# Attention's side work placed by half slots, with PSUM readers between the exponentials, and the second phase's square root moved up

## The reference, cut to what matters

```python
# block 1: attention, 16 heads of 8
zn = (z - mu) / sqrt(var + EPS) * ln_scale + ln_bias
q, k, v = split(zn @ w_qkv)
att = softmax(q @ k.T / sqrt(8))            # 512 x 512 for each head
return z + (att @ v) @ w_proj + b_proj
# block 2: quantised feed-forward
x_q = (x / s_in).astype(float8_e4m3fn)
return (x_q @ k_q * s_in * s_k).astype(bf16) + bias
# block 3: gated recurrence (convolution, gates, scan), then a gated MLP
beta = sqrt(1.0 - alpha ** 2 + 1e-06)
xs = beta * sigmoid(inp) * xc
h = associative_scan(alpha, xs)
return x + gelu(mgate) * mx @ W_shrink.T
# block 4: routing of tokens to 8 experts
```

## Time and profile before

| what | before |
|---|---|
| median of 3 runs | 1431.36 us (1431.35 to 1436.4) |
| the profiled execution | 1437.65 us |
| its span, first to last instruction | 1435.9 us |
| mean granted PE clock | 0.943 of full speed |
| PE busy | 1220.5 us (85%) |
| DVE busy | 1160.6 us (81%) |
| ACT busy | 968.2 us (67%) |
| POOL busy | 824.6 us (57%) |

### The profile page before, as it was taken

How to read it: one execution, slowest core, us unless ns; L and a number is a source line. 1 busy time by engine, 2 the same in 40 slices (tenths; PEclk the granted TensorE clock), 3 DMA queues, 4 the chain that set the end, 5 groups by cost and what they waited for, 6 DMA issues and landing times.

```text
span 1435.9 us, 26041 instructions
## 1 busy us (share of the span) xinstructions
PE 1220.5 (85%) x8624; PEld 492.4 (34%) x8624; DVE 1160.6 (81%) x2518; ACT 968.2 (67%) x1653; POOL 824.6 (57%) x1068
## 2 busy tenths in 40 slices
PE   1499899899899999999999999856999899899853
PEld 0123233233233233233233223323545545545533
DVE  2668889889889889889989988433789889889874
ACT  1177777777777777877877878555767667666630
POOL 5303554654654654655555444634677877877763
PEclk7589999999999999999999989888999999999975
DMA  1121101101101101101100100000000000000000
GB/s 56 50 83 42 35 31 42 36 31 41 37 31 42 37 31 40 38 30 41 39 30 32 34 14 3 1 0 1 1 8 16 8 8 16 8 8 16 8 8 22
DMA packets 52517, 37.87 MB, mean 26 GB/s; under 512 B 8864, under 2 KB 51744, under 8 KB 52384
## 3 DMA queue, kind: packets, MB, share of 16 engines
q1 hardware_dynamic: 52384, 36.22, 7.9%
HBM read 6.31 MB, written 4.19 MB: 7 GB/s over the span
## 4 chain that ended last, share of the span: by engine, by line
PE 33%; DVE 23%; POOL 20%; issue 13%; SPq 5%; ACT 5%; POOLq 0%; DMA 0%; ACTq 0%; DVEq 0%
DVE neg_max L473 11%; PE bank L201 10%; PE bank L182 9%; SPq L621 4%; PE bank_pair L169 4%; ACT probs L348 3%; PE bank L210 3%; POOL probs L1154 2%; PE bank L272 2%; POOL x_all L1148 2%; POOL zn L1146 1%; POOL rs_t L1088 1%; POOL probs L1119 1%; POOL rs_x L1088 1%; POOL rs_h L1116 1%
## 5 line engine op out<-in xcount | busy, mean ns | idle before, releaser
L473 DVE TENSOR_REDUCE neg_max<-bank_pair 128x2 f32<-128x1024 f32 x512 | 615.5, 1215 | 120.7 <-PE bank_pair L169 115.9
L348 ACT ACTIVATE probs<-bank 128x512 f32<-128x512 f32 x1024 | 558.5, 596 | 113.2 <-PE bank L182 108.6
L182 PE MATMUL bank<-q_stack,k_stack 50*128 50x512 bf16 x1024 | 362.3, 390 | 36.4 <-ACT probs L348 19.3
L201 PE MATMUL bank<-probs,v_pad 128*32 128x256 f32 x4096 | 331.4, 396 | 2.7 <-ACT outT L306 2.3
L169 PE MATMUL bank_pair<-k_stack,q_stack 48*128 48x512 bf16 x1024 | 293.8, 397 | 31.0 <-DMA k_stack<-k_parts 15.7
L182 PEld LDWEIGHTS bank<-q_stack,k_stack 50*128 50x128 bf16 x1024 | 83.6, 93 | 301.2 <-ACT probs L348 228.6
L201 PEld LDWEIGHTS bank<-probs,v_pad 128*32 128x32 f32 x4096 | 81.1, 108 | 175.6 <-issue 156.0
L724 PE MATMUL bank_pair<-probs,w_gates 128*128 128x512 f32 x256 | 122.7, 624 | 16.7 <-DVE probs L1046 8.9
L522 POOL TENSOR_TENSOR f_b<-f_bf,ffn_bias 128x512 bf16<-128x512 bf16 x16 | 18.9, 1182 | 157.3 <-ACT f_bf L353 157.3
L169 PEld LDWEIGHTS bank_pair<-k_stack,q_stack 48*128 48x128 bf16 x1024 | 54.0, 94 | 60.5 <-DVE neg_max L473 41.2
L1154 POOL TENSOR_TENSOR probs<-probs 128x1024 f32<-128x1024 f32 x16 | 37.7, 2354 | 62.9 <-DVE probs L1068 62.9
(11 more groups left out here) (232 smaller groups left out, 2252.6 us busy)
## 6 DMA issues: line engine op xcount, KB each, us to landing
q_stack<-q_parts SPq DMA_DIRECT2D x384, 32.0 KB
k_stack<-k_parts SPq DMA_DIRECT2D x384, 32.0 KB
x_all<-in_z_dram SPq DMA_DIRECT2D x16, 256.0 KB, 2.8
out_dram<-x_all SPq DMA_DIRECT2D x16, 256.0 KB, 2.3
q_stack<-max_rows SPq DMA_DIRECT2D x64, 8.0 KB
w_gates<-in_w_gates_dram SPq DMA_DIRECT2D x1, 512.0 KB, 3.7
w_in<-in_w_in_dram SPq DMA_DIRECT2D x1, 256.0 KB, 2.7
w_grow<-in_w_grow_dram SPq DMA_DIRECT2D x1, 256.0 KB, 3.8
```

What stands on the lines that cost most here:

```text
L182: nc.tensor.matmul(st_ps[h][:, :], k_stack[par][rows, p, c * P:(c + 1) * P], q_stack[par][rows, p, :], start=True, stop=True).then_inc(s[" ...
L201: mm = nc.tensor.matmul(acc[32 * g:32 * g + 32, cols], v_pad[bpar][:, kc, 4 * a + g, :], probs[:, at + g, cols], start=(t == 0 and kc == 0 ...
L348: nc.scalar.activation(probs[:, 4 * (n % RING) + g, :], st_ps[g % 2][:, :], ACT.Exp, scale=SCALE)\
L473: nc.vector.tensor_reduce(neg_max[j // 4][:, c, j % 4, :], score_ps[c % 2][:, :, :], AX_X, ALU.max, negate=True).then_inc(s["max_read"], 1)
```

## The change

Nothing is computed otherwise. Work is moved within the queues, and four products are cut in two.

- **PE**: side products are placed by half slot: o1 at u = 3, oT 6, proj 8 and 9 (two chunks each), maxT1 13, yT 15, ffn 16, v 17 and 18, znT 19, q 21 and 22, k 25 and 26 (256 columns each), maxT0 29, o0 31. `max_t` stands ahead of `prob_v` of its half slot.
- **ACT**: readers stand between the two exponentials of a half slot (`between`) or behind both (`behind`).
- **DVE**: the same operations in one function of `u`; `att` at 10 and the split of the maxima at 11 (before: 12 and 11), the division of o0 at 31.
- **POOL**: z_res first, then the preparation, x1, the feed-forward's bias, y, the splits of q and k, x2 last. Before: preparation, bias, z_res, x2, x1, splits, y.
- **SP**: the stack of k is issued apart from that of q, and the maxima's rows between them.
- **Second phase**: the request for the gelu table goes, and the square root stands ahead of the MLP's gelu.

```diff
+            if u == 3 and live(i, -1):
                 out_nat(1, i - 1)
+            if u in (8, 9) and live(i, -1):
+                if u == 8:
+                    wait(pe, s["oT_ready"], i - 1 + 1)
+                    wait_misc_free(pe, i, "proj")
+                tokens("proj", oT, w["proj"], (0, 1) if u == 8 else (2, 3), s["proj_ps"])
...
+            for n, first in (("q", 21), ("k", 25)):
+                if u in (first, first + 1) and live(i, 2):
+                    if u == first:
+                        wait(pe, s["znT_ready"], i + 2 + 1)
+                        if bank_of(n, i) is misc:
+                            wait_misc_free(pe, i, n)
+                    features(n, u - first)
...
         for slot in range(2 * NP):
+            for half in range(2):
+                u = 2 * slot + half
+                score_t(slot, 2 * half)
+                score_max(slot // 2, 2 * (slot % 2) + half)
+                score_t(slot, 2 * half + 1)
+                if u == 13 and live(i, 0):
+                    max_t(1, i)
+                if u == 29 and live(i, 1):
+                    max_t(0, i + 1)
+                prob_v(slot, half)
+                side_product(u)
```

```diff
         load_x(sp, i + 3)
         if live(i, 1):
-            stack_half(1, i + 1, 1 - par)
+            stack_half("q", 1, i + 1, 1 - par)
         if live(i, 0):
             max_rows_out(1, 0)
+        if live(i, 1):
+            stack_half("k", 1, i + 1, 1 - par)
         if live(i, 2):
-            stack_half(0, i + 2, par)
+            stack_half("q", 0, i + 2, par)
         if live(i, 1):
             max_rows_out(0, 1)
+        if live(i, 2):
+            stack_half("k", 0, i + 2, par)
...
-            nc.scalar.preload_act_table_set("gelu_and_others")
...
+        if live(i, -1):
+            b = i - 1
+            wait(act, s["om_ready"], b + 1)
+            A(beta, beta, ACT.Sqrt, bias=consts["tiny"][:, 0:1]).then_inc(s["beta_ready"], 1)
         if live(i, -2):
             b = i - 2
             wait(act, s["mg_ps"], b + 1)
             wait(act, s["shrink_ps"], b)
             A(grown, pair1[:, :, :], ACT.Gelu).then_inc(s["mg_ready"], 1)
```

More of the change, by code:

```diff
@@ L257, in side_product @@
                 transpose4(lambda c: zn[:, c, :], consts["ident"][:, :], misc, P, s["znT_ps"])
[L258 to L273, removed]
+            for n, first in (("q", 21), ("k", 25)):
[5 more added lines that the diff above has]
+                    features(n, u - first)
+            if u == 31 and live(i, 0):
                 out_nat(0, i)
         for slot in range(2 * NP):
[L277 to L290, removed]
+            for half in range(2):
[9 more added lines that the diff above has]
+                side_product(u)
     def scalar(act, i, par):
@@ L297, in read_max, with read_out @@
             nc.scalar.activation(max_rows[:, :], misc_bf[0:MROWS * 8, :], ACT.Copy).then_inc(s["maxT_read"], 1)
[L299 to L311, removed]
+        def read_out(u, b):
+            wait(act, s["pv_done"], 16 * b + 8 * (u + 1))
+            wait(act, s["o_ps"], 2 * (b - 1) + u + 1)
+            nc.scalar.activation(outT[u][:, :], acc[:, :], ACT.Copy).then_inc(s["acc_read"], 1)
@@ L312, in side_read, with read_v @@
+        def read_v(t):
+            if t == 0:
                 wait(act, s["v_ps"], i + 1 + 1)
                 wait(act, s["pv_done"], 16 * (i - 1) + 16)
[L314 to L318, removed]
@@ L319, in side_read, with read_hi @@
-            if slot == 4 and live(i, -1):
+            src = misc[:, :].rearrange("p (cu t g d) -> p cu t g d", t=2, g=4, d=HD)
+            dst = v_pad[1 - par][:, :, :, :].rearrange("p c (u t g) e -> p (c u) t g e", u=2, t=2)
+            nc.scalar.activation(dst[:, :, t, :, 16 * t:16 * t + HD], src[:, :, t], ACT.Copy).then_inc(s["v_ready"], 1)
+        def read_hi(n, parts):
+            wait(act, s[n + "_ps"], i + 2 + 1)
+            for half in range(2):
+                wait(act, s[f"{n}{half}_ready"], 16 * STACK_DMAS * (i + 2))
+            nc.scalar.activation(parts[:, 0, :], bank_of(n, i)[:, :], ACT.Copy).then_inc(s[n + "_hi"], 1)
@@ L320, in side_read, with read_all, between @@
+        def read_all(n, rest):
+            wait(act, s[n + "_lo"], 3 * (i + 2))
+            nc.scalar.activation(rest[:, :], bank_of(n, i)[:, :], ACT.Copy).then_inc(s[n + "_hi"], 1)
+        def between(u):
+            if u == 7 and live(i, -1):
                 wait(act, s["oT_ps"], i - 1 + 1)
@@ L328, in side_read, with behind @@
                                      scale=consts["ln_scale"][:, 0:1]).then_inc(s["znT_ready"], 1)
[L329 to L336, removed]
+            if u == 23 and live(i, 2):
+                read_hi("q", q_parts)
+            if u == 24 and live(i, 2):
+                read_all("q", q_rest)
+            if u == 27 and live(i, 2):
+                read_hi("k", k_parts)
+            if u == 28 and live(i, 2):
+                read_all("k", k_rest)
+        def behind(u):
+            if u == 1 and live(i, -1):
+                read_out(1, i - 1)
+            if u == 13 and live(i, 0):
+                read_max(1, i)
+            if u == 15 and live(i, -2):
+                wait(act, s["yT_ps"], i - 2 + 1)
+                wait(act, s["ffn_ps"], i - 2)
+                nc.scalar.activation(yT[:, :], misc_bf, ACT.Copy).then_inc(s["yT_ready"], 1)
+            if u == 17 and live(i, 0):
+                read_out(0, i)
+            if u == 18 and live(i, 1):
+                read_v(0)
+            if u == 29 and live(i, 1):
+                read_max(0, i + 1)
         for slot in range(2 * NP):
             for g in range(4):
[L340 to L343, removed]
+                u = 2 * slot + g // 2
                 if live(i, 0):
@@ L349, in scalar @@
                         .then_inc(s["exp_done"], 1)
[L350 to L355, removed]
+                (behind if g % 2 else between)(u)
     def vector(dve, i, par):
@@ L434, in between, with behind @@
+        def behind(u):
+            q = s["quant_step"]
+            b = i - 2
+            if u == 0 and live(i, -2):
                 wait(dve, q, 9 * b + 5)
@@ L436, in between @@
                     .then_inc(q, 1)
-            if slot == 2 and live(i, -2):
-                b = i - 2
+            if u == 2 and live(i, -2):
                 wait(dve, q, 9 * b + 6)
@@ L441, in between @@
                     .then_inc(q, 2)
[L442 to L443 removed]
+            if u == 8 and live(i, -2):
                 wait(dve, q, 9 * b + 8)
@@ L474, in vector @@
                                             negate=True).then_inc(s["max_read"], 1)
-                (side if c % 2 else between)(2 * p + c // 2)
+                behind(C * p + c)
     def first_stats(dve):
```

310 lines of the change are left out of this document (153 added, 157 removed).

## The result

| | before | after |
|---|---|---|
| time, median of 5 (us) | 1431.63 | 1421.62 (1414.99 to 1422.51) |
| ratio, 95% interval | | 0.991 (0.988 to 0.994) |
| profiled execution, span (us) | 1435.9 | 1420.3 |
| mean granted clock | 0.943 | 0.934 |

The forecast was 33 us of gain; about 10 came. The granted clock is the share of its full clock that PE was allowed; 0.50 is the lower of its two levels. The first views to read are the stretches, with the columns of the earlier trace rows. The first row is a full step of attention, between two copies of outT (for o1), and answers to the one there. The second and third are the two halves of step 15, the last two are steps of the second phase.

What follows compares the result with a forecast made beforehand. No engine fills the 53.59 us step, so waits between PE, ACT and DVE decide. Full steps 26, steps 14 and 15 2, start 5: 33 us off 1431.36 gives 1398, own range 1384 to 1412, wider 1378 to 1424.

Steps and rivals of the forecast that it cites:

- The start: First maxima in step -1, no longer behind the k stack: tile near 64 us; 5 us gained, between 0 and 8.
- the step: A full step of attention, by the table of half slots: 51.6 us, 2.0 less; 26 us over steps 1 to 13.
- DVE's idle time behind PE: Full attention step: DVE stands idle for 3.1 us in the table of half slots instead of 5.3.
- the wait for `att`: PE's wait of 1.4 us before the transposed maxima is gone, since `att` comes at 10, the split at 11.
- the maxima's rows: Tightest new link, ACT's copy through SP to PE's tile, 3.22 us: cost nothing, 0.5 at each as other end.
- the price of POOL beside DVE: DVE's small attention operations meeting POOL's work: 0 to 3.9 us in a step, 0.4 taken on the path.
- Rival 1: Port between DVE and POOL decides: small operations wait for whole POOL operations, step 55.1, 13 us slower, 1444; chance 0.09.
- the second phase's: Second phase with the gelu request removed and square root ahead: 0 for 13 steps, between -1 and +12 in all.
- Gelu's delay: Second phase: gelu behind two loads and the root, near 4 us behind the convolution's copies; PE's product 2.5 us later.
- Rival 2: Maxima's rows and product behind gelu late: 16 us in attention, 12 in the second phase, no change, 1426; chance 0.10.
- Steps 14 and 15: Last attention steps, lacking q and k: keep the gain from the maxima, 1 us each, 2 in all.
- The stretch between the phases: From the last outT copy to the first gate product: forecast difference 0.

Runs made afterwards that it cites:

- e2: The second phase's edit alone, attention as before, against the kernel before: 1440.3 us, ratio 1.006 (1.004 to 1.008).
- e11: The changed kernel with the square root's tables requested ahead of the convolution's copies, in ACT's idle time: 1405.9 us, ratio to the kernel before 0.983.
- e5: e1 less only the line that loads gelu's tables ahead of the convolution's copies: 1419.0 us, ratio to the kernel before 0.992.
- e1: The attention part of the change, with the second phase put back as before, against the kernel before: 1408.6 us, ratio 0.986 (0.983 to 0.988).

## Why the forecast was wrong

**Right.** The start (first tile forecast near 64 us, seen at 62.56), the step (51.6 forecast, 51.4 seen), DVE's idle time behind PE (3.1 and 3.1), the wait for `att` gone, next to no wait for the maxima's rows in a full step (0.2 us at one weight load), the price of POOL beside DVE small on the whole (the two `y_absmax` operations took 0.17 and 0.25 us, 0.15 and 0.16 before). Rival 1, the port, did not decide, though `y_q` took 1.40 us for its 0.67 of before, as forecast for one that meets POOL. The Trainium skill (SBUF — State Buffer, "Who interferes with whom") states that a DVE instruction with two SBUF inputs contends with a POOL instruction that reads SBUF, and the trace agrees with these 1.40 us.

**The step that failed** is the second phase's: "I take 0 for 13 steps, between -1 and +12". It measured 9.5 us between the two profiles. It cost 9 us alone (e2) and 10 to 14 against a version with the load hidden (e11). Gelu's delay was worked out well (3.8 us behind the copies against 4 forecast, PE's wait 1.6 to 2.4 against 2.5). Two things were missed. The removed load was priced by where it lay, in idle time; what counts is where the next load then lies, on the path of ACT's last readers (e5). And slack was counted as if a wait within it were free: it is in time, but PE's product behind it ran at 1.2 GHz in four steps, 1.5 to 1.6 us more each, and no term of the sum had a clock in it. Rival 2 named 12 us for it, nearly the size, by another mechanism (0.9 in each step), with 0.10 of chance.

**Steps 14 and 15** were taken as a gain of 2 us, and this failed too. At the full clock on both sides the old attention took 48.5 and 42.8 us (e2), the new one 50.3 and 44.6 (e1): 3.6 us longer. In step 14 of e1 the end is what grew: the half slots at u = 29 and 31 took 2.70 and 3.39 us against 1.65 and 1.96 in a full step, with `y_q` at 1.75. The gain of a full step was carried over to steps that lack q and k without a table of their own. The rest of the +7.4 in the first table is the clock, in step 15 of after and in step 14 of before.

**The stretch between the phases** was taken as 0: +4.5 in e1. Of these 2.6 lie in its chain. 1.2 come from its first part, that now runs through DVE's setup, division, att and x1 (19.9 us to `bn_c`, 18.7 before), and 1.4 from two DVE operations with POOL at work beside them (`y_sum` and one L1054 at 1.42 us, 0.70 and 0.76 before). The rest are PE's products at a lower clock.

**The sum.** By the two spans the forecast missed 17 us: 9.5 in the second phase, 9.4 in steps 14 and 15, 1.6 between the phases, less 3.2 that the start, the full steps and the end gave beyond it. By the medians it missed 23, for the profiled execution of before lay 6 us above the median of its kernel. 1421.6 lies outside the forecast's own 1384 to 1412. That it lies inside the wider 1378 to 1424 is luck: more than half of the miss came from steps 14 and 15 and from between the phases, where a gain or nothing was forecast, with no range of their own.

## What to carry to other kernels

Before taking out a table load that lies in idle time, find the next instruction that needs other tables, and put the load's time there: 1.28 us on the chain of last readers was worth some 10 over 15 steps. Where an engine has slack, price the wait twice, once in time and once in what its clock does behind it. A step at the edge of a loop, which lacks part of the work, wants a table of its own. In a loop where one engine makes tiles for another, put a reader where the first engine has its next tile free already (behind the second exponential), and try the opposite placement on the same table of half slots before calling the order's gain its ceiling.

## What the hardware showed beside

- The same wait of PE, 2.38 us in the same place of each step, was followed by a product at full clock in some steps and at half in others of one execution (1.98 and 3.60 us). The clock's fall is not a fixed price of a wait. It came at even distances: in e2 every third step (products at 1136.3, 1218.3 and 1300.2), in e5 every second.
- A shorter wait can stand ahead of a slow product too: 0.96 and 0.38 us in e5 came before products at a mean clock of 0.70. They took 1.5 us longer, but the step only 0.4.
- With identical attention code, step 15 took 44.6 us or 50.7 as the granted clock was 1.00 or 0.55 in its second half.
- A switch of tables took 1.28 us and 0.02 around it (1192.26 to 1193.56, with the instruction before ending at 1192.24). The Trainium skill (ScalarE: Activation LUTs, "What ACT_TABLE_LOAD costs") has 1283 ns for the load, which agrees, and a drain of some 1380 ns with it, which no switch here shows.
